# Scaling a finished expert tile by its gates on ScalarE in place of VectorE

## What is computed

```python
top_p, top_i = jax.lax.top_k(probs, K)                       # K = 2 of E = 4
gates = zeros((T, e)).at[arange(T)[:, None], top_i].add(top_p / sum(top_p))
h = silu(einsum('td,edf->etf', xf, w1)) * einsum('td,edf->etf', xf, w3)
expert_out = einsum('etf,efd->etd', h, w2)                   # D = 256, F = 1024
out = einsum('te,etd->td', gates, expert_out)
x = x + tanh(g_ffn[0]) * out
```

## Time and profile before

| | |
|---|---|
| median of 3 runs | 528.44 us (528.23 to 528.6) |
| the profiled execution, time | 529.63 us |
| its span in the trace | 527.8 us |
| mean granted TensorE clock | 0.963 of full speed |
| busy: PE / DVE / ACT / POOL | 493.0 / 402.8 / 304.9 / 183.2 us |
| matmuls L1719 (up), three groups | 110.7 + 108.6 + 108.6 us on `ps_scores` |
| DVE weight subtractions L1335 / L1331 | 104.1 / 43.9 us |
| gate scaling L1363, 35 instructions | 0.478 us each |

### The profile page before, as it was taken

The page is one execution under the profiler, slowest core; times in us unless marked ns, Lnnn a source line. Parts: engine busy times, 40 slices in busy tenths (PEclk is TensorE's granted clock), DMA queues, the critical chain, the costliest instruction groups (busy, mean ns, idle before and its releaser), DMA issues.

```text
span 527.8 us, 11417 instructions
## 1 busy us (share of the span) xinstructions
PE 493.0 (93%) x3630; PEld 446.6 (85%) x3630; DVE 402.8 (76%) x955; ACT 304.9 (58%) x724; POOL 183.2 (35%) x190
## 2 busy tenths in 40 slices
PE   9999999997996999999999999999999999999991
PEld 7556777775775899899999989999999999998880
DVE  2588888994895488888788888888878878887660
ACT  3025556544444466578656665676667667766650
POOL 1445657368648103453024452122112201222111
PEclk9979999996995899999999999999999999999996
DMA  8999883001101311312201321221122102211110
GB/s 272 357 392 392 356 329 129 20 21 52 52 22 49 94 43 42 63 24 62 39 12 32 83 43 41 41 42 21 22 42 41 20 20 30 30 21 21 21 11 11
DMA packets 32392, 45.13 MB, mean 85 GB/s; under 512 B 9709, under 2 KB 28781, under 8 KB 32109
## 3 DMA queue, kind: packets, MB, share of 16 engines
q1 hardware_dynamic: 24807, 34.66, 19.3%
q0 software_dynamic: 6576, 8.92, 10.0%
q10 hardware_dynamic: 960, 0.94, 0.6%
HBM read 33.50 MB, written 21.82 MB: 105 GB/s over the span
## 4 chain that ended last, share of the span: by engine, by line
PE 54%; DVE 24%; issue 7%; ACT 5%; POOL 5%; DVEq 1%; DMA 1%; ACTq 0%; SPq 0%; POOLq 0%
PE ps_scores L1719 16%; PE ps_wide L1739 6%; DVE w_lo L1335 5%; PE ps_misc L1739 5%; PE ps_probT L1719 5%; PE ps_wide L1556 4%; DVE w_lo L1331 3%; DVE hid_lo L1344 2%; DVE ps_scores L1340 2%; PE ps_misc L1501 2%; PE ps_scores L1527 2%; PE ps_misc L1578 2%; PE ps_scores L1768 2%; ACT hid_hi L937 2%; POOL score L1052 2%
## 5 line engine op out<-in xcount | busy, mean ns | idle before, releaser
L1119 POOL DMA_INDIRECT out_x<-y_out,meta x35 | 57.4, 1640 | 207.6 <-DVE y_out L1363 202.5
L1335 DVE TENSOR_TENSOR w_lo<-w,w_hi 128x512 fp32r<-128x512 f32 x152 | 104.1, 686 | 15.4 <-ACT w_hi L916 7.9
L1719 PE MATMUL ps_scores<-xt_hi,w_hi 128*128 128x256 f32 x384 | 110.7, 288 | 0.2 <-DVE xt_lo L1349 0.2
L1719 PE MATMUL ps_scores<-xt_lo,w_hi 128*128 128x256 f32 x384 | 108.6, 283 | 0.0
L1719 PE MATMUL ps_scores<-xt_hi,w_lo 128*128 128x256 f32 x384 | 108.6, 283 | 0.0
L916 ACT CAST w_hi<-w 128x512 fp32r x152 | 95.3, 628 | 3.5 <-issue 3.1
L1719 PEld LDWEIGHTS ps_scores<-xt_hi,w_hi 128*128 128x128 f32 x384 | 73.6, 192 | 0.9 <-DVE xt_lo L1349 0.5
L1719 PEld LDWEIGHTS ps_scores<-xt_lo,w_hi 128*128 128x128 f32 x384 | 73.6, 192 | 0.0
L1719 PEld LDWEIGHTS ps_scores<-xt_hi,w_lo 128*128 128x128 f32 x384 | 73.6, 192 | 0.0
L937 ACT CAST hid_hi<-ps_scores 128x256 fp32r<-128x256 f32 x96 | 35.8, 373 | 57.5 <-DVE ps_scores L1340 56.1
L1052 POOL TENSOR_TENSOR score<-score,lowest 128x616 f32<-128x616 f32 x32 | 38.9, 1217 | 56.1 <-DVE lowest L1210 55.8
(11 more groups left out here) (238 smaller groups left out, 1234.6 us busy)
## 6 DMA issues: line engine op xcount, KB each, us to landing
grouped<-in_pad SPq DMA_DIRECT2D x1, 10296.0 KB
w<-in_L_ffn_w SPq DMA_DIRECT2D x8, 1024.0 KB, 12.4
w2s<-in_L_ffn_w SPq DMA_DIRECT2D x4, 1024.0 KB, 13.7
xg<-grouped SPq DMA_DIRECT2D x16, 256.0 KB, 2.7
out_x<-xall SPq DMA_DIRECT2D x8, 256.0 KB, 2.1
xall<-in_x SPq DMA_DIRECT2D x1, 1024.0 KB, 13.2
xall<-in_x SPq DMA_DIRECT2D x1, 768.0 KB, 7.7
ctxT<-in_ctx_t SPq DMA_DIRECT2D x2, 308.0 KB, 5.4
```

What stands on the lines that cost most here:

```text
L1119: pool.indirect_dma_start(out, bass.IndirectOffsetOnAxis(ap=meta[:, s % 2, t, E:E + 1].bitcast(U32), axis=0), y_out[:, s % 2, t, :], None, ...
L1335: dve.tensor_tensor(w_lo[:, f % NB], unit_weights(e, f), w_hi[:, f % NB].bitcast(F32), ALU.subtract).then_inc(w_lo_done, 1)
L1719: mm = pe.matmul(ps_gu[f % NB][:, m, 0:n], lhs, rhs[:, a, c, 0:n], start=(k == 0), stop=(k % (3 * DC) == 3 * DC - 1), skip_group_check=True)
```

## The change

`scale`, with its two helpers, goes from DVE's program to ACT's. The operation is the same, one instruction per block of 128 rows: DVE's `tensor_scalar` with a multiply by a per-partition gate becomes ACT's `activation` with the function Copy and that gate as its scale. It waits for the same three semaphores and counts up the same one. Its place in the slot is unit 1 again, now behind ACT's `hidden_hi` (in half tiles behind `weights_hi`). The read of the previous expert's number at the start of slots 1 to 18 goes with it. The scaling of the last tile, at the very end, moves as well. Nothing changes in PE's, POOL's and SP's programs.

```diff
@@ act @@
+                def scale(s, a, e):
+
+                    act.wait_ge(down_done, FC * (s + 1))
+                    if isinstance(s, int):
+                        act.wait_ge(meta_in[a], 16 * (s // 2 + 1))
+                    else:
+                        act.wait_ge(meta_in[a], meta_turn(s, a))
+                    if not (isinstance(s, int) and s < 2):
+
+                        act.wait_ge(added[a], added_turn(s, a))
+                    for t in range(tiles_of(s)):
+                        gate_of = meta[:, a, t, bass.ds(e, 1)]
+                        act.activation(y_out[:, a, t], ps_y[a][:, t], ACT.Copy, scale=gate_of).then_inc(y_scaled, 1)
+
+                def meta_turn(s, a):
+                    return 8 * (s + (2 - a))
+
+                def added_turn(s, a):
+                    return added_by(s) if isinstance(s, int) else 16 * (s - a)
+
                 def slot(s, a):
-                    last, n = is_slot(s, SLOTS - 1), tiles_of(s) * P
+                    first, last, n = is_slot(s, 0), is_slot(s, SLOTS - 1), tiles_of(s) * P
+                    if not first:
+                        e_before = expert_of(act, s - 1)
                     e = expert_of(act, s)
...
                         hidden_hi(u, f, n)
+                        if f == 1 and not first:
+                            scale(s - 1, 1 - a, e_before)
                         if f == 5 and not last:
                             x_hi(s + 1, 1 - a)
...
                 def short(s, a):
                     last = s == SLOTS - 1
+                    e_before = expert_of(act, s - 1)
                     e = expert_of(act, s)
...
                             weights_hi(u + AHEAD, e_after, f + AHEAD - FC)
+                        if f == 1:
+                            scale(s - 1, 1 - a, e_before)
                         if f == 5 and not last:
                             x_hi(s + 1, 1 - a)
                     if last:
                         inner_copy(s, FC - 1)
+                        scale(s, a, e)
@@ dve @@
-                def scale(s, a, e):
...
-                        dve.tensor_scalar(y_out[:, a, t], ps_y[a][:, t], gate_of, None, ALU.mult).then_inc(y_scaled, 1)
...
                 def slot(s, a):
-                    first, last, n = is_slot(s, 0), is_slot(s, SLOTS - 1), tiles_of(s) * P
-                    if not first:
-                        e_before = expert_of(dve, s - 1)
+                    last, n = is_slot(s, SLOTS - 1), tiles_of(s) * P
                     e = expert_of(dve, s)
...
-                        if f == 1 and not first:
-                            scale(s - 1, 1 - a, e_before)
...
                 def short(s, a):
                     last = s == SLOTS - 1
-                    e_before = expert_of(dve, s - 1)
                     e = expert_of(dve, s)
...
-                        if f == 1:
-                            scale(s - 1, 1 - a, e_before)
...
                 run_slots(slot, short)
-                scale(SLOTS - 1, (SLOTS - 1) % 2, expert_of(dve, SLOTS - 1))
```

## The result

The changed kernel takes 521.98 us, the median of 4 runs (520.61 to 524.47), against 528.34 (526.66 to 528.6, 4 runs) before. The ratio is 0.9879, 95% interval 0.9852 to 0.9907. The forecast was 522.6 with a range of 520.2 to 525.5. The profiled run of the changed kernel took 522.42 us with a span of 519.9.

A forecast was written before the change was run, and what follows sets the result against it. PE bounds the late tiles, while in tiles 1 to 7 and the half tiles PE waits for DVE. 3.7 (scaling) + 1.2 - 0.3 (loads) + 1.2 (half tiles) = 5.8 us off 528.44: 522.6 us, range 520.2 to 525.5.

The forecast's parts named there:

- The scaling: Tiles 1, 2 and 4 to 7: moving the pair off DVE, worth 0.78 us on its path, saves 3.7 us in all.
- ACT's room in tiles 2 and 7: Before hid_hi of unit 2: 0.99 us of room for a 0.76 pair, so about 0.3 of 0.78 us arrives.
- The price on ACT: One scaling on ACT takes 0.47 us, 0.38 after overlap, so 0.76 a pair; upper end 1.02.
- The register loads: Tile starts: one load fewer on DVE gives 1.2 us in tiles 4 and 6; ACT's extra load costs 0.3.
- 0.1 each: Starts of tiles 1, 5 and 7: ACT's extra load pushes hid_hi some 0.15 us late, charged 0.1 us per tile.
- tile starts longer than before: A sign that the forecast is wrong: tiles begin with longer starts than in the kernel before; no size given.
- tiles 4 and 6 shorter by 1.2 or more: A sign that the forecast is right: these two tiles shrink by at least 1.2 us, tiles 1 and 5 by 0.7.
- tiles 9 to 15 all at 17.71 or 17.72: Late tiles: PE has no idle time, so DVE's work costs nothing; they should still take 17.7 us.
- The half tiles: Three half tiles at the end: 0.6 us from a load and 3 x 0.2 from scaling, 1.2 in all, between 0.3 and 1.4.
- the whole stall of 0.80: First half tile: PE waits 0.80 us for a DVE product behind two register loads; one fewer gives 0.6.
- ACT as the next bound: Rival: pair costs 1.02 us, load its full 0.5 at every start, half tiles give only 0.3; 525.3 us, chance 0.19.
- The table reload: Rival: Copy with a scale needs another activation table, two loads of 1.283 us per tile; about 540 us, chance 0.03.

The follow-up runs named there:

- scale_only: Changed kernel with register loads left as before: DVE still reads both numbers, ACT keeps the previous one, only the scaling moves; 524.00 us, ratio 0.9899.
- act_early: Changed kernel with ACT's pair of scalings ahead of hid_hi of unit 1 instead of behind it; 521.63 us, ratio 0.9860.
- held_dve: Kernel before the change, scaling still on DVE, but DVE keeps the previous expert's number in unrolled tiles instead of loading it again; 525.62 us, ratio 0.9943.
- pair_twice: Changed kernel with each scaling done twice on ACT, first into a spare tile nobody reads; 530.76 us, ratio 1.0043.
- half_on_dve: Changed kernel with scaling and register load of the half tiles, and the last scaling, given back to DVE; 522.30 us, ratio 0.9890.
- shift_dve: Kernel before the change with eight tiny memsets of a spare tile on DVE ahead of the first expert tile; 531.02 us, one execution.
- all_held: Changed kernel without any register load at the start of tiles 1 to 8 and half tiles, on ACT and DVE; 522.29 us, ratio 0.9855.
- held_act: Changed kernel with ACT keeping the previous expert's number in unrolled tiles instead of loading it again; 520.76 us, ratio 0.9864 against the kernel before.
- held_early_pe: Changed kernel without tile-start loads on ACT and DVE, scaling ahead of hid_hi, PE's half-tile load behind its first up product; 518.63 us, ratio 0.9811.
- shift_act: Kernel before the change with eight tiny copies into a spare tile on ACT ahead of the first expert tile; 529.05 us, one execution.

## Why the prediction was right, and where it was not

**The scaling.** 3.7 us in the tiles was forecast, 3.68 measured (scale_only). By tile: 0.78, 0.3, 0.3 for tiles 1, 2 and 7, measured 0.77, 0.36, 0.32. Tiles 4, 5 and 6 gave 0.65, 0.23 and 1.18 for a forecast of 0.75, 0.78 and 0.78, and tile 8 another 0.16, so the exact match of the sum is partly luck. The rule behind it held too: whole where ACT has more room than the pair needs, cut to ACT's room in tiles 2 and 7. act_early is its test: an emptier place on ACT gave those tiles, and no others, 0.36 and 0.54 more. The price on ACT, 0.47 and 0.76 for a pair, came out as 0.480 and 0.72.

**The register loads.** The net was forecast at +0.9 (+1.2 - 0.3) and is 0.85 (after against scale_only). Both sides of it were mis-sized: this is the step of the prediction that failed, DVE's freed load put at nothing in the plain tiles and ACT's new one at "0.1 each". DVE's freed load is worth 2.65 us alone (held_dve, tiles 0 to 8), not 1.2, because it helps in the plain tiles as well (0.44, 0.23, 0.39 in tiles 1, 5, 7), where I had hidden it under a weight subtraction. ACT's new one costs 1.26, not 0.3, above all in tiles 1 and 7 (0.52 and 0.68). A load of 0.5 less 0.23 to 0.26 of idle time leaves 0.24 to 0.27; the prediction says 0.15 and charges 0.1, and gives no reason for either. And it read the idle time at the wrong place. The load stands ahead of the tile's first silu, so it delays the silu, with it the w2 cast behind it and DVE's product, and the idle time in front of hid_hi, which is a wait for that same product, absorbs none of it: ACT's idle time before the silu went from 0.25 to 0.78 us. That is also the sign "tile starts longer than before", which the prediction had named for being wrong. The two faults cancel in tiles 1 and 7, whose net of 0.71 and 0.20 was forecast as 0.68 and 0.2. This part of the forecast came out right by luck.

**How the gains of tiles 4 to 6 land.** The signs named tiles 4 and 6 shorter by 1.2 or more and tile 5 by about 0.7. Measured: 0.71, 2.15 and 0.23. In tile 4 PE is busy for all of 18.42 us and tile 5 is at 17.71, so what DVE gained there is lead, and tile 6, the next one where DVE falls behind, takes it. The sum is what counts: 1.35 + 0.68 + 1.38 = 3.41 by the terms (scaling and load of each), 3.09 measured. The rest I put down to PE's floor, the time that PE alone needs for a tile. The same floor is why the parts don't add: 3.68 for the scaling and 2.65 for DVE's load, less 1.26 for ACT's, would be 5.07 us, and 4.53 came. In tile 4 the scaling alone gave 0.65 and the load alone 0.72, but both together 0.71, with PE busy throughout. (The prediction also has tiles 9 to 15 all at 17.71 or 17.72; tile 15 takes 17.49 or 17.50 in every kernel but pair_twice.)

**The half tiles.** 1.2 us was forecast and 1.92 measured. The term nearly stands in its sum: half_on_dve gives back 1.13, as 0.54 + 0.26 + 0.33 for the three half tiles, against 0.8 + 0.2 + 0.2. The first of them was mis-sized: one load less brings DVE's first product 0.36 us closer to hid_lo (1.43 in half_on_dve, 1.07 in after), and not 0.6. The stall at the first half tile is gone as a whole: PE waited 0.80 before the turn and now starts it 0.06 after the matmul before it ends, and the idle time of PEld fell from 1.01 to 0.26. In the kernel after, timeline of DVE and PE:

```profile
474.99 0.29 DVE L1401 TENSOR_TENSOR act_g<-act_g,ps_scores 128x128 f32<-128x128 f32 x1
...
475.33 0.14 PEld L1773 LDWEIGHTS ps_scores<-small,act_g 128*128 128x128 f32 x1 [0.26 <-DVE act_g L1401]
475.34 0.33 PE L1773 MATMUL ps_scores<-small,act_g 128*128 128x128 f32 x1
```

DVE's product has no idle time before it any more. The other 0.79 us are not in my sum. 0.57 of them lie in half tile 1 (1.11 gained, 0.54 given back by half_on_dve) and 0.26 in the last part (0.59 and 0.33); counted up to PE's last product, which leaves out the end, it is 0.31 (0.55 and 0.24). That goes with the pause of 0.28 before the last silu, which before has and half_on_dve doesn't. In half tile 1 the late first register load delays DVE's first product by 0.39 (1.82 against 1.43 after hid_lo), of which 0.2 to 0.4 showed in the half tile's own time under shift_dve; 0.2 to 0.4 of the 0.57 stay without a cause. The forecast took the whole stall of 0.80 to be two loads and gave 0.6 for one of them, when part of it was a load that began late. That both pauses need nothing of this change is shown by the two shifts. What in the chip makes them is open.

**The rivals.** ACT as the next bound was right as a mechanism and wrong in size in the kernel after, where it costs tiles 2 and 7 some 0.9 us (act_early). With twice the work the whole gain is gone: 530.76 us. The table reload didn't occur. The late tiles stayed at 17.7.

**What stays open.** Why tiles 9, 11 and 13 lengthen in pair_twice, why the half tiles of all_held are 0.74 us longer than those of held_act, why tile 2 still takes 19.85 and tile 1 18.00 us in held_early_pe, 2.1 and 0.3 above the late tiles (the prediction counted most of that as PE waiting for DVE), and the mechanism of the shifts.

## What to carry to other kernels

Price a moved instruction by the idle time of the new engine at that place, down to the next result that others wait for, and not by its share of the span: here a pair at 0.72 us fitted, two pairs did not, and one place earlier would have fitted better. Count what travels along with it: the register load that went with the scaling was worth 2.65 us on the engine it left, taken alone, and cost 1.26 on the other (0.85 net once the scaling had moved), and the kernel that keeps the numbers in registers (held_early_pe) beats both. Where a second engine waits for the first in every unit, charge a delay in full, and look for slack at the first instruction behind the delay: idle time further down may be a wait for the very work that is delayed.

## What the runs showed of the hardware

A register load of an index by an engine's own sequencer takes about 0.5 us (0.298 + 0.190 on DVE, where two start 0.6 apart), and taking one away saved 0.4 to 0.7 us in each of tiles 1, 4, 6 and 7 (held_dve) and tiles 1 and 7 (held_act). Pauses of 0.28 and of 0.39 us vanished when eight tiny instructions were put in 280 us earlier on the engine that had them (shift_act, shift_dve), and over the thirteen traces they stand just where an 8 KB transfer of instructions starts close behind (1.22 us after hid_lo, 0.64 to 0.91 after the last silu), and are missing where none does.

The attention stage's length goes with the granted clock, and that differs between executions of the same code. Stretches 0 to 60 and 120 to 180 us of before and, under them, of pair_twice, whose first tile starts earliest (180.89):

```profile
0.00:60.00 60.00, 54.49 (x271) 38.87 (x272) 38.77 (x98) 20.13 (x41) 24.74 (x31) 0.94 1.01 357
120.00:180.00 60.00, 50.35 (x298) 40.83 (x299) 38.30 (x96) 25.89 (x58) 38.72 (x43) 0.80 0.16 54
```

```profile
0.00:60.00 60.00, 54.01 (x293) 39.16 (x294) 41.17 (x103) 21.90 (x45) 27.93 (x36) 1.00 1.02 358
120.00:180.00 60.00, 49.75 (x313) 40.76 (x314) 40.07 (x97) 27.33 (x60) 36.25 (x41) 0.86 0.17 57
```

The granted clock is 0.94 and 0.80 in the one, 1.00 and 0.86 in the other, where 1.00 is 2.4 GHz and 0.50 is 1.2. Over all thirteen traces the clock of the first 60 us orders the starts: 1.00 in the two that start at 180.89 and 181.47, 0.94 in the eight from 182.56 to 184.28, 0.91 in the three from 184.95 to 185.43. Whether the lower clock makes the stage longer or a wait makes both is not tested. In the tiles the granted clock is 1.00 in every window shown. So the spread of up to 4.5 us between these traces sits in the first third of the kernel, and one execution's whole time says less than its feed-forward stage.
